# Attention scores as 16-bit pairs in two row halves of TensorE

## The reference

```python
y = x * rsqrt(mean(x * x) + RMS_EPS) * rms_w
y = einsum('bsm,cm->bsc', y, w_in)          # queries 2048, keys 512, values 512
q, k = rope(q), rope(k)
qk = einsum('bghsd,bgxpd->bghsp', q, k) * 64 ** -0.5
attn = softmax(where(causal, qk, -inf))
o = einsum('bghsp,bgxpd->bghsd', attn, v)
x = layernorm(x + (x + einsum('bsc,mc->bsm', o, w_out)))
x = layernorm(x + ffn(x))
```

## Time and profile before

| | us |
|---|---|
| median of three runs | 1426.91 (1426.64 to 1427.55) |
| span of the profiled execution | 1425.4 |
| TensorE products busy | 1318.0 (92%) |
| TensorE weight loads busy | 838.4 (59%) |
| VectorE busy | 1147.2 (80%) |
| ScalarE busy | 1116.3 (78%) |
| GpSimd busy | 873.7 (61%) |

### The profile page before, as it was taken

The page is one execution under the profiler, slowest core; times in us unless marked ns, Lnnn a source line. Parts: engine busy times, 40 slices in busy tenths (PEclk is TensorE's granted clock), DMA queues, the critical chain, the costliest instruction groups (busy, mean ns, idle before and its releaser), DMA issues. The chain is left out here.

```text
span 1425.4 us, 25329 instructions
## 1 busy us (share of the span) xinstructions
PE 1318.0 (92%) x7328; PEld 838.4 (59%) x7328; DVE 1147.2 (80%) x3062; ACT 1116.3 (78%) x2327; POOL 873.7 (61%) x905
## 2 busy tenths in 40 slices
PE   4689999999999999999999999999999999898886
PEld 2456565665656565665656565666656566565554
DVE  4578887878887888878887888878788787887976
ACT  4768878788888888788887878788887888787664
POOL 1266667386645766386646766387646767786565
PEclk9799999999999999999999999999999999999998
DMA  6101111011101211021101211021100211210002
GB/s 199 27 20 38 64 30 31 27 57 45 37 21 45 59 29 31 23 60 44 36 24 26 72 35 31 23 60 43 38 24 23 75 35 37 61 42 27 18 33 85
DMA packets 45163, 61.82 MB, mean 43 GB/s; under 512 B 10464, under 2 KB 27104, under 8 KB 45024
## 3 DMA queue, kind: packets, MB, share of 16 engines
q1 hardware_dynamic: 45024, 60.20, 14.3%
HBM read 34.74 MB, written 4.46 MB: 27 GB/s over the span
## 5 line engine op out<-in xcount | busy, mean ns | idle before, releaser
L1100 DVE SCALAR_TENSOR_TENSOR prob_lo<-t,prob_hi 128x512 f16<-128x512 f32 x576 | 394.7, 686 | 76.0 <-ACT prob_hi L797 72.2
L797 ACT ACTIVATE prob_hi<-t 128x512 f16<-128x512 f32 x576 | 340.2, 591 | 146.1 <-PE t L1221 140.8
L1165 PE MATMUL s<-k_t,q_t 128*128 128x512 f32 (+3 forms) x1536 | 428.2, 383 | 23.8 <-DVE neg_max L1009 8.5
L829 ACT ACTIVATE prob<-prob,neg_max 128x896 f32<-128x896 f32 (+7 forms) x512 | 392.0, 767 | 7.2 <-DVE neg_max L1009 4.3
L1221 PE MATMUL t<-ident,prob 128*128 128x128 f32 x2304 | 350.8, 275 | 6.9 <-ACT prob L829 6.8
L1221 PEld LDWEIGHTS t<-ident,prob 128*128 128x128 f32 x2304 | 290.6, 143 | 109.7 <-ACT prob L829 13.2
L1009 DVE CUSTOM_DVE_ANT_0 prob<-s,mask 128x512 f32<-128x512 f32 (+3 forms) x512 | 289.6, 583 | 53.4 <-PE s L1165 33.3
L1165 PEld LDWEIGHTS s<-k_t,q_t 128*128 128x128 f32 x1536 | 244.9, 193 | 66.4 <-DVE neg_max L1009 19.0
L1136 PE MATMUL ot<-prob_lo,v_sb 128*128 128x512 f16 x576 | 221.0, 384 | 27.1 <-DVE prob_lo L1100 27.0
L1134 PE MATMUL ot<-prob_hi,v_sb 128*128 128x512 f16 x576 | 223.9, 389 | 0.9 <-DVE o_raw L1081 0.9
L770 POOL TENSOR_TENSOR o_lo<-o_raw,o_hi 128x256 f16<-128x256 f32 x128 | 86.2, 674 | 198.7 <-ACT o_hi L907 196.9
(11 more groups left out here) (106 smaller groups left out, 1841.4 us busy)
## 6 DMA issues: line engine op xcount, KB each, us to landing
swapped<-flat SPq DMA_DIRECT2D x320, 64.0 KB, 2.0
spread<-recip_rows SPq DMA_DIRECT2D x128, 128.0 KB
recip_rows<-turned SPq DMA_DIRECT2D x512, 0.5 KB
raw<-L_attn_w_in SPq DMA_DIRECT2D x8, 768.0 KB, 4.2
raw<-L_attn_w_out SPq DMA_DIRECT2D x8, 512.0 KB, 3.6
out<-acc SPq DMA_DIRECT2D x16, 256.0 KB, 2.0
acc<-L_attn_x SPq DMA_DIRECT2D x3, 1024.0 KB, 10.4
acc<-L_attn_x SPq DMA_DIRECT2D x4, 256.0 KB, 4.2
```

The costliest lines, as they stand in the source:

```text
L797: act.activation(prob_hi[:, u % 2, :], t_ps[u % 2][:, :], ACT.Copy, scale=P_SCALE).then_inc(prob_hi_done, 1)
L829: act.activation(row, row, ACT.Exp, bias=neg_max[:, kk % 4, h:h + 1], scale=-1.0, accum_out=total[:, kk % 4, h:h + 1]).then_inc(ex_done, 1)
L1100: dve.scalar_tensor_tensor(out=prob_lo[:, u % 2, :], in0=t_ps[u % 2][:, :], scalar=P_SCALE, in1=prob_hi[:, u % 2, :], op0=ALU.mult, op1=AL ...
L1165: mm = pe.matmul(s_ps[:, off:off + cols], q_t[:, h, s * P:(s + 1) * P], k_t[:, part, keys:keys + cols], start=(part == 0), stop=(part == 1))
```

## The change

Queries and keys become pairs of 16-bit parts. `q_t` holds, for each pair of heads, the high part in one plane and the low part in another, each head in its own 64 rows; `k_t` keeps its shape in 16 bits. A score step of an odd head does nothing on TensorE any more; the step of the even head makes both heads: three products each (high-high, high-low, low-high), the two heads in rows 0 to 63 and 64 to 127 in turn, into the two banks. It waits until `max_done` has reached n, so until both banks are emptied. VectorE still empties each head's bank at the places of both. Since 16-bit parts have to stay in range, the projection is copied to `flat` with the constant scale V_SCALE, and the true scale is applied when a bank is emptied, read from `score_scale`. The query parts are made by one instruction of 128 x 512 where there were two of 64 x 512, on ScalarE and on GpSimd (VectorE in the opening); the key's two stay.

```diff
+S_SCALE = -DH ** -0.5 / V_SCALE ** 2
...
-        q_t = sb("q_t", [P, HG, NT * P], F32R)
-        k_t = sb("k_t", [P, 2, 12 * P], F32R)
+        q_t = sb("q_t", [P, 2, HG // 2, NT * P], F16)
+        k_t = sb("k_t", [P, 2, 12 * P], F16)
...
-                                pool.tensor_tensor(q_t[DH:P, 2 * c, at], x[0:DH, :], q_t[0:DH, 2 * c, at].bitcast(F32),
-                                                   ALU.subtract).then_inc(part_lo, 1)
-                                wait(pool, part_lo, g, CHUNKS, n + 1)
-                                pool.tensor_tensor(q_t[0:DH, 2 * c + 1, at], x[DH:P, :],
-                                                   q_t[DH:P, 2 * c + 1, at].bitcast(F32), ALU.subtract
+                                pool.tensor_tensor(q_t[:, 1, c, at], x[:, :], q_t[:, 0, c, at], ALU.subtract
                                                    ).then_inc(parts_done, 1)
...
-                            group, kind = (g + b // 2) % 2, c // 2
-                            wait(act, flat_scale_done, g, 1, 1 + b // 2)
-                            act.activation(flat[:, n % 2, :], bank[:, :], ACT.Copy,
-                                           scale=flat_scale[:, group, kind:kind + 1]).then_inc(flat_done, 1)
+                            act.activation(flat[:, n % 2, :], bank[:, :], ACT.Copy, scale=V_SCALE).then_inc(flat_done, 1)
...
-                                act.activation(q_t[0:DH, 2 * c, at], x[0:DH, :], ACT.Copy)
-                                act.activation(q_t[DH:P, 2 * c + 1, at], x[DH:P, :], ACT.Copy).then_inc(parts_hi, 1)
+                                act.activation(q_t[:, 0, c, at], x[:, :], ACT.Copy).then_inc(parts_hi, 1)
...
+                            group = (g + b // 2) % 2
+                            wait(dve, score_scale_done, g, 1, 1 + b // 2)
...
-                                                     scale=-DH ** -0.5, scalar=low_max[:, h:h + 1] if c else 3e38,
+                                                     scale=score_scale[:, group:group + 1],
+                                                     scalar=low_max[:, h:h + 1] if c else 3e38,
...
-                                dve.reciprocal(flat_scale[0:DH, n, 1:2], wy_scale[0:DH, :])
-                                dve.reciprocal(flat_scale[:, n, 0:1], wy_scale[:, :]).then_inc(flat_scale_done, 1)
+                                dve.reciprocal(wy_back[:, n:n + 1], wy_scale[:, :]).then_inc(wy_back_done, 1)
+                                wait(dve, wy_back_done, g, 1, 2)
+                                dve.tensor_scalar(score_scale[:, n:n + 1], wy_back[:, n:n + 1], wy_back[:, n:n + 1],
+                                                  S_SCALE, ALU.mult, ALU.mult).then_inc(score_scale_done, 1)
...
                             _, b, s, h, c = e
+                            if h % 2:
+                                continue
+
                             n = scored(b, s, h, c)
-                            cols, off = min(BANK, (s + 1) * P - c * BANK), n % 2 * BANK
-                            keys = k_slots(b, c) * P
+                            cols, keys = min(BANK, (s + 1) * P - c * BANK), k_slots(b, c) * P
                             wait(pe, parts_done, g, CHUNKS, chunk(b, s // HALF, h // 2) + 1)
-                            wait(pe, max_done, g, STEPS_MADE, n - 1)
-                            for part in range(2):
-                                mm = pe.matmul(s_ps[:, off:off + cols], q_t[:, h, s * P:(s + 1) * P],
-                                               k_t[:, part, keys:keys + cols], start=(part == 0), stop=(part == 1))
-                            mm.then_inc(sc_full, 1)
+                            wait(pe, max_done, g, STEPS_MADE, n)
+                            for m, (q_part, k_part) in enumerate(((0, 0), (0, 1), (1, 0))):
+                                for odd in range(2):
+                                    rows = slice(odd * DH, (odd + 1) * DH)
+                                    mm = pe.matmul(s_ps[:, odd * BANK:odd * BANK + cols],
+                                                   q_t[rows, q_part, h // 2, s * P:(s + 1) * P],
+                                                   k_t[rows, k_part, keys:keys + cols], start=(m == 0), stop=(m == 2))
+                                    if m == 2:
+                                        mm.then_inc(sc_full, 1)
```

More of the change, by code:

```diff
@@ L326, in seq_block @@
         rms_s = sb("rms_s", [P, 2, KC])
-        flat_scale = sb("flat_scale", [P, 2, 2])
+        wy_back = sb("wy_back", [P, 2])
+        score_scale = sb("score_scale", [P, 2])
         out_scale = sb("out_scale", [P, 2])
@@ L369, in seq_block @@
         scales_done = sem("scales_done")
-        flat_scale_done = sem("flat_scale_done")
+        wy_back_done = sem("wy_back_done")
+        score_scale_done = sem("score_scale_done")
         o_scale_done = sem("o_scale_done")
@@ L616, in _ @@
             pool.memset(sums[:, 1, 1:2], 1.0).then_inc(ones_set, 1)
-            pool.memset(flat_scale[:, :, 1], V_SCALE).then_inc(ones_set, 1)
             pool.memset(recip[:, :, :], 0.0).then_inc(consts_set, 1)
@@ L751, in one @@
                                 at = k_half(b, half)
-                                pool.tensor_tensor(k_t[0:DH, 1, at], x[0:DH, :], k_t[0:DH, 0, at].bitcast(F32),
+                                pool.tensor_tensor(k_t[0:DH, 1, at], x[0:DH, :], k_t[0:DH, 0, at],
                                                    ALU.subtract).then_inc(part_lo, 1)
-                                wait(pool, part_lo, g, CHUNKS, n + 1)
-                                pool.tensor_tensor(k_t[DH:P, 1, at], x[0:DH, :], k_t[0:DH, 0, at].bitcast(F32),
+                                wait(pool, part_lo, g, CHUNKS // 3, n // 3 + 1)
+                                pool.tensor_tensor(k_t[DH:P, 1, at], x[0:DH, :], k_t[0:DH, 0, at],
                                                    ALU.subtract).then_inc(parts_done, 1)
@@ L972, in events @@
                             if c < 2:
[L973 to L976, removed]
+                                dve.tensor_tensor(q_t[:, 1, c, at], x[:, :], q_t[:, 0, c, at], ALU.subtract
                                                   ).then_inc(parts_done, 1)
@@ L979, in events @@
                                 at = k_half(b, half)
-                                dve.tensor_tensor(k_t[0:DH, 1, at], x[0:DH, :], k_t[0:DH, 0, at].bitcast(F32),
+                                dve.tensor_tensor(k_t[0:DH, 1, at], x[0:DH, :], k_t[0:DH, 0, at],
                                                   ALU.subtract).then_inc(part_lo, 1)
-                                dve.tensor_tensor(k_t[DH:P, 1, at], x[0:DH, :], k_t[0:DH, 0, at].bitcast(F32),
+                                dve.tensor_tensor(k_t[DH:P, 1, at], x[0:DH, :], k_t[0:DH, 0, at],
                                                   ALU.subtract).then_inc(parts_done, 1)
@@ L1032, in events @@
                                 wait(dve, scales_done, g, 2, 4)
-                                if plan is first:
-                                    dve.wait_ge(ones_set, 3)
-                                dve.reciprocal(flat_scale[0:DH, n, 1:2], wy_scale[0:DH, :])
-                                dve.reciprocal(flat_scale[:, n, 0:1], wy_scale[:, :]).then_inc(flat_scale_done, 1)
+                                dve.reciprocal(wy_back[:, n:n + 1], wy_scale[:, :]).then_inc(wy_back_done, 1)
+                                wait(dve, wy_back_done, g, 1, 2)
+                                dve.tensor_scalar(score_scale[:, n:n + 1], wy_back[:, n:n + 1], wy_back[:, n:n + 1],
+                                                  S_SCALE, ALU.mult, ALU.mult).then_inc(score_scale_done, 1)
                         elif e[0] == "wo":
@@ L1045, in events @@
                                 wait(dve, o_back_done, g, 1, 1)
-                                wait(dve, flat_scale_done, g, 1, 1)
-                                dve.tensor_scalar(out_scale[:, g % 2:g % 2 + 1], flat_scale[:, g % 2, 0:1], o_back[:, :],
+                                wait(dve, wy_back_done, g, 1, 1)
+                                dve.tensor_scalar(out_scale[:, g % 2:g % 2 + 1], wy_back[:, g % 2:g % 2 + 1], o_back[:, :],
                                                   0.5 / V_SCALE, ALU.mult, ALU.mult).then_inc(out_scale_done, 1)
@@ L1183, in events @@
                                 pe.wait_ge(rms_squared, 1)
-                                pe.wait_ge(ones_set, 3)
+                                pe.wait_ge(ones_set, 2)
                             if n == 0:
```

## The result

| | before | after |
|---|---|---|
| median, us | 1427.0 | 1583.0 |
| ratio to before | | 1.109 (1.107 to 1.111) |
| span of the profiled execution | 1425.4 | 1580.2 |
| TensorE idle in the 825 us from 265 to 1090 | 28.5 | 109.0 |

The account below looks back on a forecast made before the run. TensorE's issue was taken as the bound, VectorE some 12% behind. From 1426.9 us: +52 net for wait and saving, +6 edges, -1 opening, -12 idle time gave 1472 us (+3.2%), range 1385 to 1560.

Parts of the forecast that it names:

- the single loop: From one narrow pair's scores through both emptyings to the next pair's scores: 1.88 us against 1.28 before.
- TensorE's own work for scores: Score products on TensorE: from 284 us to 194 with halves side by side, so TensorE sheds 90 us.
- Rival 3: Score products: the row halves don't run beside each other, time 1654 us; chance 0.08.
- the bound with six slots, 377: Score products on TensorE if halves don't overlap: 377 us over all four widths, 93 more than before.
- The edges: TensorE changing between row halves and whole array, 719 times: 0.01 us each, +6 us in the loop count.
- Rival 2: Each edge of the score blocks costs the product's tail, 0.17 us: +101 instead of +6, 1567 us; chance 0.14, in-between cases included.
- The new wait: Scores wait for both banks: loop longer in 140 pairs by 104 us, 52 saved in 243 others, net +52.
- The cruder count: Second bank emptied after the next pair's present start in 245 of 383 pairs, 174 us; upper end, +84.
- What comes back: TensorE's present idle time, some 49 us in the whole: a quarter, 12 us, taken off; between 0 and 49.
- VectorE: Emptyings reading the score scale through a pointer: 0.06 us longer each, 31 to 47 us more busy time.
- ScalarE and GpSimd: Query copies and subtractions halved: 40 us less on ScalarE, 80 on GpSimd; only 1 us counted, at the opening.
- Rival 1: The wait for both banks hides and the kernel is faster: 1385 us (1370 to 1420); chance 0.25.

Follow-up runs that it names:

- the kernel with 128 rows: The changed kernel with each head at its own place, waiting for its own bank, three 16-bit products of 128 rows, no edges: 1475.2 us, ratio 1.034.

## Why the prediction was wrong

The sign, the mechanism (the wait for both banks) and the single loop were right; the sum was 111 us short. Two steps failed: that in the pairs outside the loop TensorE keeps its saving, and the price of an edge, taken at a tenth of what it is. By its steps:

- **TensorE's own work for scores.** The halves do run side by side: 0.75 us for a 512-wide pair, of which 0.65 are slots, as forecast. Rival 3 falls. (The 128-wide slot was taken at 0.09 and is 0.056, 6 us in all; the bound with six slots, 377, had it at some 0.06, and would be 388 with the 0.09 used beside it.)
- **The edges.** This is the first term mis-sized: 0.01 us was taken, 0.10 measured, within the bounds of 0.01 and 0.17. I took the end nearest to a row that was no change of row form at all, a late weight load. Put into the same loop count, 0.095 and the narrower 128-wide slot give +103 instead of +58, so this accounts for 45 us. It also takes most of the gain that the change was made for: a 512-wide pair with both its edges costs TensorE 0.75 + 0.53 - 0.44 = 0.84 us against 0.93 before, where the forecast had 0.65. Rival 2's price (0.17) was as far off on the other side; that its 1567 lies near 1583 is luck, as the main loss is the wait. The Trainium skill (TensorEngine Tiling (Array Packing), Key Properties) says that changing the tiling mode drains TensorE. The trace agrees, with 0.31 against 0.216, but what it costs is less than a product's whole tail of 0.17. (The prediction calls this the third rival's rule; it is the second's.)
- **The new wait.** With the edge set right, I compared each pair's distance in the two traces. In the 147 pairs whose loop was then longer than the old distance, the count gives 116 us, and 131 were measured: the loop holds pair by pair. In the other 236 the count has TensorE keeping 14 us of savings, and they lost 26. That is the step that failed: "in the other 243 TensorE keeps its saving". Two things stand in its place in the trace. 58 of these pairs did wait for a bank, 38 us in all against 3 before; that fits VectorE coming to the emptyings late with work from before the pair, which the loop leaves out, but no run isolates it. And the time at the 1.2 GHz level in these pairs is 76 us against 32, which can be up to 22 of the missing 40; the prediction had no term for the clock. As a whole the wait was put too low: the sum's +52 beside 90 us saved means 142 for the wait, and alone it cost 186. The cruder count in the prediction, 174 us of second banks emptied after the next pair's present start, was nearer, though it was made with other TensorE times.
- **What comes back.** 12 us were taken off, and nothing was left to come back: TensorE's idle time went from 28.5 to 109 in 825 us. These four, 45 + 15 + 40 + 12, make up the 111 us that were missing. Where TensorE stayed the bound, as in the kernel with 128 rows, some did: 20 of the 91 us by its idle time.
- **VectorE.** 0.06 for the pointer was right, also for the second one. As part of the path it is 26 us.
- **ScalarE and GpSimd.** They are 50 and 94 us less busy, where 40 and 80 were forecast; the row for GpSimd is also 0.12 shorter each (1171 against 1287). That nothing of it counts in the time was forecast; no run isolates it.
- **Rival 1** fails by its own condition: the wait had to cost under some 50 us and cost 186.

The terms in the end, with what measured them: the wait 186 (alone, on the kernel before), and the rest of the change against it -31. Of that rest the pointer is +26, so halves, formats and shorter copies are -57, and the format alone gave -25 in the kernel before; the edges lie within it at up to 719 x 0.10 = 72. Those parts were measured in different kernels and need not add up to the microsecond. How much of the 72 lies on the path in the changed kernel, where TensorE often waits anyway, was not separated.

## What to carry to other kernels

When two results are made together, their buffers must be free together: look at when the consumer (here VectorE) frees the later one, in its own order, against when the producer (TensorE) starts today. Count that lateness over all pairs before counting the producer's saving, and move the consumer's two steps beside each other first. Take the cheap part of such a change by itself: here the 16-bit format alone was a gain, and the pairing a loss.

## What the runs showed of the hardware

Products of 64 rows in different halves run beside each other, and out of their written order: three of one head followed by three of the other take three slots and an edge, 0.76 us, not five or six slots. Going between 64-row and 128-row products costs TensorE 0.09 to 0.11 us each way in the rows, 0.101 by the time of a whole kernel with 1001 of them (clock and idle time included). A second pointer operand in VectorE's custom instruction costs the same 0.06 us as the first (745 - 683 and 805 - 746 ns). A 512-column product of 16 bits takes 0.216 us a slot where the 32-bit form takes 0.93 / 4 = 0.23. Ten times in 825 us the granted clock fell to its 1.2 GHz level at or just behind a wait of 2.1 us of TensorE, and 512-column products then start 0.427 us apart; the kernel before, whose waits there stay under 1.5 us, shows no fall in that stretch.
